# Moving half of a projection block in front of the row pass in every step of an attention schedule

## The reference, cut to what matters

```python
x = x + attn_a(layernorm(x))      # gated linear recurrence
x = x + ffn(layernorm(x))         # ternary weights
x = x + attn_b(layernorm(x))      # softmax attention: the part that the change touches
x = x + ffn(layernorm(x))

def attn_b(x, Wq1, Wq2, Wk, Wv, Wlam, Wo):        # 16 heads of 32 channels
    q = concat([heads(x @ Wq1), heads(x @ Wq2)])   # 32 query heads
    k2, v2 = repeat(heads(x @ Wk), 2), repeat(heads(x @ Wv), 2)
    scores = where(causal, q @ k2.T / sqrt(32), min)
    p = softmax(scores)
    y1, y2 = split(p @ v2)
    y = y1 - sigmoid(x @ Wlam) * y2
    return merge_heads(y) @ Wo
```

## Time and profile before

| what | value |
|---|---|
| median of three runs | 2132.3 us |
| profiled execution | 2131.86 us, span 2130.0 us |
| TensorE busy | 2035.2 us, 96% of the span |
| VectorE, ScalarE, GpSimd busy | 60%, 40%, 42% of the span |
| attention, units 0 to 13 | 833 to 1658 us of the span |
| attention, units 14 and 15 | 1658 to 1764 us |

### The profile page before, as it was taken

One profiled execution on the slowest core, in us unless ns is written; L12 is line 12 of the kernel. 1 busy time (PEld: TensorE's weight loads), 2 busy tenths in 40 slices (PEclk: granted clock), 3 DMA queues, 4 the chain that ended last, 5 costly groups with the idle time before them and its releaser, 6 DMA issues.

```text
span 2130.0 us, 29410 instructions
## 1 busy us (share of the span) xinstructions
PE 2035.2 (96%) x11824; PEld 902.1 (42%) x11824; DVE 1271.8 (60%) x1838; ACT 855.3 (40%) x1304; POOL 888.4 (42%) x457
## 2 busy tenths in 40 slices
PE   7998999999999999999999999999999879899999
PEld 3444444444444445343434334343433323444444
DVE  5868687647746634455555555555556623775634
ACT  4434353334434322434443434344344442443431
POOL 3766585600000001666666666766766681000000
PEclk9999999999999999999999999999999999999999
DMA  7111110300000011000001010000000101000001
GB/s 232 35 30 35 30 36 30 129 15 1 1 1 1 1 48 26 1 16 14 18 11 21 5 27 1 16 16 16 2 11 6 61 30 40 1 1 20 21 1 40
DMA packets 68999, 55.53 MB, mean 26 GB/s; under 512 B 36800, under 2 KB 55232, under 8 KB 68608
## 3 DMA queue, kind: packets, MB, share of 16 engines
q1 hardware_dynamic: 61952, 41.07, 6.6%
q10 hardware_dynamic: 6912, 12.59, 2.0%
HBM read 43.02 MB, written 10.62 MB: 25 GB/s over the span
## 4 chain that ended last, share of the span: by engine, by line
PE 53%; DVE 4%; ACT 3%; POOL 3%; issue 1%; DVEq 0%; ACTq 0%; POOLq 0%
PE psum L116 9%; PE psum L1151 8%; PE psum L1239 8%; PE psum L1300 6%; PE psum L1283 5%; PE psum L140 5%; PE psum L1189 3%; POOL b_totals L1524 2%; PE psum L1279 2%; PE psum L1245 2%; PE psum L1257 2%; DVE b_maxima L1587 2%; PE psum L1270 1%; PE psum L1197 1%; ACT b_probs L1446 1%
## 5 line engine op out<-in xcount | busy, mean ns | idle before, releaser
L1524 POOL TENSOR_TENSOR b_totals<-b_totals,b_probs 128x2048 f32<-128x2048 f32 (+3 forms) x160 | 515.4, 3221 | 311.1 <-ACT b_probs L1446 304.9
L1587 DVE TENSOR_REDUCE b_maxima<-psum 128x2 f32<-128x1024 f32 (+3 forms) x384 | 350.6, 954 | 392.4 <-PE psum L1245 232.9
L1446 ACT ACTIVATE b_probs<-psum 128x1024 f32<-128x1024 f32 (+3 forms) x320 | 228.6, 765 | 256.4 <-PE psum L1283 233.1
L435 PE MATMUL psum<-hT,a_win 128*128 128x512 f32 x640 | 293.1, 601 | 0.8 <-ACT hT L555 0.8
L116 PE MATMUL psum<-hT,b_early 128*128 128x512 f16 x1024 | 228.2, 383 | 5.2 <-DVE b_middle L202 5.2
L116 PE MATMUL psum<-hT,W 128*128 128x512 f16 x1024 | 226.4, 381 | 3.9 <-DVE a_win L202 3.9
L435 PEld LDWEIGHTS psum<-hT,a_win 128*128 128x128 f32 x640 | 120.4, 193 | 130.8 <-issue 129.5
L116 PEld LDWEIGHTS psum<-hT,b_early 128*128 128x128 bf16 x1024 | 100.2, 98 | 131.5 <-issue 10.6
L116 PEld LDWEIGHTS psum<-hT,W 128*128 128x128 bf16 x1024 | 100.4, 98 | 126.5 <-DVE a_win L202 7.6
L1501 POOL MEMSET b_mask<- 128x128 f32 x1 | 0.2, 204 | 356.8 <-POOLq L267 356.8
L1634 DVE RECIPROCAL b_down<-b_down 128x128 f32<-128x128 f32 x128 | 111.9, 918 | 40.7 <-ACT b_down L1424 40.7
(11 more groups left out here) (225 smaller groups left out, 3285.0 us busy)
## 6 DMA issues: line engine op xcount, KB each, us to landing
a_parts<-in_w_guT ACTq DMA_DIRECT2D x32, 256.0 KB, 2.8
ternary<-W SPq DMA_DIRECT2D x1, 6144.0 KB, 18.1
a_win<-in_w_inT SPq DMA_DIRECT2D x20, 256.0 KB, 7.2
a_parts<-in_w_pT ACTq DMA_DIRECT2D x16, 256.0 KB, 2.6
b_down<-lam_rows SPq DMA_DIRECT2D x32, 128.0 KB, 2.7
b_early<-ternary SPq DMA_DIRECT2D x8, 512.0 KB, 7.8
out<-x SPq DMA_DIRECT2D x16, 256.0 KB, 2.2
x<-in_x SPq DMA_DIRECT2D x3, 1024.0 KB, 7.3
```

The source lines that it names most:

```text
L435: last = pe.matmul(ring(s, j), win[:, at:at + P], core["hT"][:, (i * KT + k) * BLK:(i * KT + k + 1) * BLK], start=(k == 0), stop=(k == KT ...
L1446: act.activation(held(u, s)[:, 2 * a:2 * a + 2, off:BLK], pair_banks(("score", u, s, a))[:, :, off:BLK], ACT.Exp, scale=SCALE).then_inc(ex ...
L1524: pool.tensor_tensor(acc, acc, held(u, s)[:, :, off:BLK], ALU.add).then_inc(summed, 1)
L1587: dve.tensor_reduce(maxima[u % 2][:, :].rearrange("p (h q c) -> p h q c", h=HPT, q=QT)[:, 2 * a:2 * a + 2, qt, kc], pair_banks(("row", u, ...
```

## The change

`FILL_BEFORE_ROWS` names the steps in which the part at place 0 is issued ahead of the row pass. In all other steps both parts stand behind the row. Before, these were steps 0 and 4; now they are all twelve, of which six more hold a part: 1, 3, 6, 7, 8 and 9.

```diff
 OUT_AT = [{9: 2, 11: 3}, {10: 0, 11: 1}]
-FILL_BEFORE_ROWS = (0, 4)
+FILL_BEFORE_ROWS = tuple(range(NS))
 NORM_AT = {(3, 0): 0, (4, 0): 1, (6, 0): 2, (7, 0): 3}
```

## The result

Four runs of the changed kernel have a median of 2153.73 us (2153.5 to 2155.76), four of the kernel before one of 2131.03 us (2129.67 to 2132.58). The ratio is 1.0105, 95% interval 1.0093 to 1.0118: the change costs 22.7 us, with 19.8 to 25.1 inside the interval. Forecast were 19.4 us, 2151.3 us against a range of 2143 to 2158. The profiled execution took 2155.76 us with a span of 2153.9 us.

A forecast was written before the change was run, and what follows sets the result against it. TensorE, running almost without a hole in the attention, was taken as the bound. Units 0 to 13 add 18.2 us and unit 14 adds 1.2, so 19.4 on 2131.86 gives 2151.3 us, range 2143 to 2158.

The forecast's parts named there:

- split: TensorE fills on both sides of the row instead of together: 1.05 + 1.06 against 1.92 us, +0.19 for changing matmul shape.
- wait removed: Fill in front covers the row's wait for the exponential of score pair 0: row 1.07 instead of 1.32 us, -0.25.
- wait added: Next step's second score pair waits for the maximum of row pair 0: scores 1.51 instead of 1.19 us, +0.32.
- The two pages: TensorE skill pages: prefetched weights would make splits free, lowering the sum 15.2 us; tiling-mode changes drain TensorE, which the forecast followed.
- Steps 6 to 9: Moved fills in these attention steps: +0.26, +0.03, +0.26 and +0.15 us, the last +0.50 in odd units.
- Steps 1 and 3: Moved fills there cost +0.15 us each; 0.35 more behind step 1 in odd units, hidden under key copies in even ones.
- Unit 0: First attention unit, without output in step 9: forecast 1.35 us longer.
- Unit 14: Unsplit norm jobs moved ahead of the row in steps 3, 6 and 7: forecast +1.2 us, bounds 0 and 3.
- In step 3 the maximum is short: 0.05: Unit 14, step 3: moving the norm job ahead of the row was to cost only 0.05 us.
- The two rival courses of unit 14: VectorE and GpSimd miss each other, 2145 us (8%), or a second such pair meets or the clock falls, 2158 (7%).
- price of step 6: Moving step 6's first fill ahead of its row: +0.19 - 0.25 + 0.32 = +0.26 us per unit.
- One bound of the prediction: Mask stall of 0.35 us, 14 times, taken between 0.25 and 0.45: -1.5 to +1.5 us on the sum.

The follow-up runs named there:

- e1: Kernel before, with the first fill put in front of the row in step 6 too; step 6 -0.05, step 7 +0.06 us, 0.00 a unit.
- e2: Kernel before, with both fills of step 6 unsplit in front of the row; step 6 -0.36, step 7 +1.22, +0.86 us a unit.
- e4: Changed kernel with VectorE's row maximum reading only half the columns; span 2125.7 us, +0.33 us a unit against e3.
- e3: Kernel before with VectorE's row maximum reading only half the columns; span 2119.3 us, 10.7 less than before.
- e5: Kernel before, with the first fill in front of the row in step 7 too; ratio 0.9996 (0.9987 to 1.0006), +0.04 us a unit by trace.
- e6: Kernel before, with the first fill in front of the row in steps 6 and 7 too; +0.30 us a unit by trace.
- e10: The changed kernel run once more, unaltered; 2153.4 us against 2130.41 for the kernel before, ratio 1.0102 (1.0089 to 1.0116).

## Why the prediction was right, and where it was off

- **The three prices** (split 0.19, wait removed 0.25, wait added 0.32) came back in the changed kernel: 1.06 + 1.06 against 1.92, row 1.07 against 1.32, scores 1.50 against 1.19. The split's price is shown by e1 and e2, where the same four matmuls of step 6 take 1.05 + 1.06 on the two sides of the row and 1.91 together in front of it, and by e4 against e3; the added wait's cause by e2 (its place moved with the row) and e3/e4 (it went with the reduction's length).
- **The two pages.** The Trainium skill's "TensorE: Matmul & The Clock Gate", Part 2, would have the next weights loaded under the running matmul, and the split free. The trace disagrees: with the waits for the maximum gone, the six splits of a unit less the row waits that they hide should cost 6 x 0.19 - 3 x 0.25 - 3 x 0.03 = 0.30, and +0.33 was measured (e4 against e3). "TensorEngine Tiling (Array Packing)", Key Properties, with its drain at a change of mode, fits. So does a plain comparison in the trace of before: four such fills take 1.92 from start to start when scores (32 rows) come next, 1.82 before the bf16 mask in the full shape, and 1.77 before the output, which has their shape and type (1235.50 in the earlier trace rows to the line below). So a boundary alone costs little, another type 0.05 more, and another shape on top of that 0.10. No run here looked inside the 0.19.

```profile
1237.27 1.88 PE L1257 MATMUL psum<-b_wo,b_down 128*128 128x512 f32 x4
```

- **Steps 6 to 9.** Forecast +0.26, +0.03, +0.26, +0.15 (+0.50 in odd units). Read with the wait at its cause: +0.26, +0.03, +0.27, +0.16 (+0.51).
- **Steps 1 and 3.** Forecast +0.15 with 0.35 more behind step 1 in odd units and none in even ones: +0.16, +0.36 and 0.00. The key copies on ScalarE hide the late scores of step 2 in even units, as the earlier trace rows had it.
- **Unit 0** was 0.24 over. Its step 2 has no `den` job, so the late row of step 2 has no fill behind it, and step 3's scores, which the forecast held free, wait 0.13. Another 0.04 is in step 1, whose row had no wait to lose (1.31 before, 1.30 now), the rest is spread over steps 6 to 9.
- **Unit 14** was mis-sized: 1.2 forecast, 1.7 to 1.9 measured. The moved jobs of steps 6 and 7 came as forecast in sum, 1.18 against 1.17 and 1.35 (steps 6 to 8 together, in the two traces), but in part by luck: step 7's job alone gave 0.4 instead of 0.58 (e5), and in e6 step 6's added 1.0 to that instead of 0.6. The term that failed is "In step 3 the maximum is short: 0.05"; steps 3 to 5 grew by 0.55. Short it is, but a `norm` is the step's only fill, and with it in front nothing stands between row and scores (1697.89 to 1698.65), so even a reduction of 256 columns holds their second pair, till 1699.13, 0.48 behind the first:

```profile
1697.89 0.50 PE L1239 MATMUL psum<-b_middle 32*128 32x128 f32 x8
...
1698.65 0.39 PE L1279 MATMUL psum<-b_middle,b_ones_b 32*128 32x512 bf16 x2
...
1699.13 0.39 PE L1279 MATMUL psum<-b_middle,b_ones_b 32*128 32x512 bf16 x2
```

- **The two rival courses of unit 14** did not come: the long subtraction on VectorE still lasts 3.95 in the changed kernel (from 1706.96).
- **What the forecast did not see** is that its price of step 6 holds only together with step 7's. It charged step 6 with the late scores of step 7 in full. That was right because step 7's own fill had moved as well; had the change been step 6 alone, the same working would have given +3.4 us, and the trace says 0.1 over units 0 to 12 (e1). So that part of the sum came out right for a reason that the prediction does not give.
- **The sum** is 19.0 + 1.8 = 20.8 us by the traces, 19.4 forecast. The timed 22.7 has 20.8 in its interval; the 1.9 between is not assigned to anything, and e10 has it again (23.0, interval 19.0 to 24.7). One bound of the prediction is misadded: 14 x 0.10 is 1.4, not 1.5.

None of the versions beats the kernel before by anything that can be measured. Steps 0 and 4 are those in which the hidden row wait (0.87) pays for the split and for what comes behind. In steps 6 to 8 the wait is 0.25: it covers the split of 0.19, but not the held scores as well (one step alone: 0.00, +0.04, +0.27).

## What to carry to other kernels

Filler put in front of a consumer hides that consumer's wait, but it is taken from behind it, where it hid the wait of whoever needs the consumer's result; compare both distances with both latencies (here 2.46 from scores to the row's second pair, 2.46 from the row to the next scores' second pair). A wait in one step may be the cushion for lateness from the step before, so prices of single moves don't add: read the pair of steps. And a split into shapes that alternate has its own price, here 0.19: the wait that it hides must pay for that and for the wait that it lays bare behind. 0.87 did, 0.25 did not.

## What the runs showed of the hardware that was not expected

- **When the clock falls is not fixed by the code, and all that follows is shifted.** Twelve traces, with the same instructions ahead of the attention, begin it between 831.5 and 835.7 us. TensorE's granted clock (1.00 is 2.4 GHz, 0.50 the lower level of 1.2 GHz) shows where. From 405 to 415 us it is 0.83 in the trace of before and 0.66 in that of the changed kernel, and one and the same ScalarE instruction (L156) starts at 424.55 in the one and 426.08 in the other. By 762 us the lateness is 1.85 of the later 2.46. e10 is as late there (1.84), but from 821 to 836 us its clock is 0.77, where the two others have 0.66, and it begins the attention 1.7 sooner than the first trace of the same kernel. The lines are before's, the changed kernel's first trace twice, and e10's:

```profile
405.00:415.00 10.00, 6.66 (x26) 2.61 (x24) 5.28 (x7) 2.02 (x4) 4.33 (x3) 0.83 0.61 157
...
405.00:415.00 10.00, 6.66 (x19) 2.29 (x17) 5.11 (x6) 1.23 (x2) 4.32 (x3) 0.66 0.61 157
821.00:836.00 15.00, 11.93 (x53) 8.00 (x53) 7.52 (x16) 0.06 (x1) 2.04 (x2) 0.66 0.00 0
...
821.00:836.00 15.00, 11.94 (x66) 7.57 (x67) 7.51 (x16) 1.71 (x2) 2.04 (x2) 0.77 0.01 1
```

- **The same in unit 14**, where step 1 took 0.9 us longer in two traces and step 2 about 1.5 longer in four others, across kernels that don't differ there. In each of the six the granted clock of just that step is 0.74 or 0.75; in the six other traces it is 1.00 in both steps. Step 6 of unit 14, with the same order in both, took 9.00 in e1 at a granted clock of 0.81 and 10.28 in the changed kernel's first trace at 0.70; the 1.7 to 1.9 us above compare traces with 0.67 to 0.70 there. Step 1 in the changed kernel's first trace and in e10:

```profile
1683.80:1690.60 6.80, 5.97 (x40) 1.94 (x38) 1.82 (x2) 4.54 (x6) 0.61 (x1) 0.75 0.00 0
...
1682.10:1688.00 5.90, 4.87 (x41) 1.62 (x38) 1.82 (x2) 4.56 (x6) 0.59 (x1) 1.00 0.00 0
```

- **Work of the same shape side by side is cheaper**: row straight into scores (e2) took 0.97 from start to start, row into a fill 1.07, with the same matmuls in the row.
